# Two reordered attention blocks with half of their zero products, and a third whose exponentials read PSUM

## The reference, cut to what matters

```
# layers 0 and 2: 16 heads of 8 dimensions, keys and values from the 77 context tokens
Q = (x @ Wq.T).reshape(B, xN, 16, 8)
attn = softmax(einsum('bqhd,bkhd->bhqk', Q, K) * SCALE)
O = einsum('bhqk,bkhd->bqhd', attn, V).reshape(B, xN, 128)
return O @ Wo.T

# layer 3, first attention: 16 heads of 32 dimensions, keys and values from x itself (128 tokens)
a = softmax(einsum('bhsd,bhtd->bhst', q, k) * D ** (-0.5))
a = a * mask          # after the softmax: later keys only
o = einsum('bhst,bhtd->bhsd', a, v)
x_out = x + o @ li1_w + li1_b
```

## Time and profile before

| what | value |
|---|---|
| median of 3 runs | 5575.47 us (5569.66 to 5575.83) |
| the profiled execution's own time | 5589.97 us |
| its span, first to last instruction | 5588.1 us |
| busy, share of the span: PE, PEld | 87%, 64% |
| busy: DVE, ACT, POOL | 71%, 48%, 39% |
| mean granted TensorE clock | 0.936 of full speed |

### The profile page before, as it was taken

The page is one execution under the profiler, slowest core; times in us unless marked ns, Lnnn a source line. Parts: engine busy times, 40 slices in busy tenths (PEclk is TensorE's granted clock), DMA queues, the critical chain, the costliest instruction groups (busy, mean ns, idle before and its releaser), DMA issues. The chain is left out here.

```text
span 5588.1 us, 132733 instructions
## 1 busy us (share of the span) xinstructions
PE 4842.0 (87%) x41659; PEld 3572.6 (64%) x41659; DVE 3953.4 (71%) x9897; ACT 2700.3 (48%) x5454; POOL 2176.0 (39%) x3095
## 2 busy tenths in 40 slices
PE   7888998999952799688889989889898899998898
PEld 4555667888852466455566667767776677776554
DVE  5666876777766333677767768989886789897544
ACT  4545774555530233454555545555553455554344
POOL 5443001100027100776533357777776433333200
PEclk9989999999975899899999999999998999999878
DMA  1002400000011333100100000000000000000000
GB/s 40 8 7 66 209 0 6 5 5 5 5 56 44 114 135 133 35 23 22 30 2 0 0 6 0 0 0 0 0 0 7 3 2 2 2 2 7 0 14 17
DMA packets 109012, 141.38 MB, mean 25 GB/s; under 512 B 35832, under 2 KB 83256, under 8 KB 103996
## 3 DMA queue, kind: packets, MB, share of 16 engines
q1 hardware_dynamic: 100544, 120.88, 6.3%
q0 software_dynamic: 8192, 16.79, 1.0%
HBM read 47.44 MB, written 58.72 MB: 19 GB/s over the span
## 5 line engine op out<-in xcount | busy, mean ns | idle before, releaser
L2213 POOL TENSOR_TENSOR l3a_probs<-l3a_probs,l3a_later 128x512 f32<-128x512 f32 x256 | 320.6, 1280 | 4.9 <-DVE l3a_total L2401 4.9
L2199 POOL TENSOR_TENSOR l3a_keys<-l3a_kT,head 128x2048 f32<-128x2048 f32 x64 | 230.4, 3600 | 232.2 <-ACT l3a_kT L2326 232.2
L181 POOL TENSOR_TENSOR l1x_ve<-l1x_mv,eps 128x1 f32<-128x1 f32 x64 | 12.2, 190 | 646.7 <-DVE l1x_mv L173 646.7
L2261 PE MATMUL l3a_scores<-l3a_keys,l3a_qT 128*128 128x512 f32 x512 | 255.5, 601 | 4.2 <-POOL l3a_keys L2199 4.2
L1696 POOL TENSOR_TENSOR l2f_hid<-l2f_prod,l2f_route 128x512 f32<-128x512 f32 x128 | 152.1, 1193 | 254.7 <-DVE l2f_prod L1843 251.3
L309 PE MATMUL l3a_po<-l3a_vals,l3a_probsT 128*128 128x32 f32 x2048 | 251.0, 271 | 0.1
L309 PEld LDWEIGHTS l3a_po<-l3a_vals,l3a_probsT 128*128 128x128 f32 x2048 | 250.2, 194 | 0.4 <-ACT l3a_probsT L290 0.4
L265 ACT ACTIVATE l3a_probs<-l3a_probs 128x512 f32<-128x512 f32 x256 | 161.7, 632 | 180.7 <-DVE l3a_probs L256 175.7
L1582 PE MATMUL l1e_h<-l1e_xhi,l1f_parts 128*128 128x512 f16 x640 | 205.1, 382 | 9.7 <-DVE l1e_gated L1640 8.2
L2199 POOL TENSOR_TENSOR l3c_keys<-l3c_kT,head 128x1232 f32<-128x1232 f32 x64 | 144.0, 2250 | 156.7 <-ACT l3c_kT L2326 156.7
L295 DVE SCALAR_TENSOR_TENSOR l1x_loT<-l1x_turned,l1x_hiT 77x512 f16<-77x512 f32 x256 | 168.9, 679 | 48.9 <-ACT l1x_hiT L288 48.9
(11 more groups left out here) (581 smaller groups left out, 17155.9 us busy)
## 6 DMA issues: line engine op xcount, KB each, us to landing
l_rows<-l0f_zeros SPq DMA_DIRECT2D x34, 1024.0 KB, 27.1
l1f_parts<-l1f_split SPq DMA_DIRECT2D x40, 512.0 KB, 3.6
l1e_x_in<-l_rows SPq DMA_DIRECT2D x40, 256.0 KB, 2.8
l1f_down<-l1f_w SPq DMA_DIRECT2D x40, 256.0 KB, 2.4
l_rows<-l1e_y_out SPq DMA_DIRECT2D x40, 256.0 KB, 2.7
l1f_w<-in_L_W SPq DMA_DIRECT2D x16, 256.0 KB, 3.6
out_x<-x_res SPq DMA_DIRECT2D x16, 256.0 KB, 2.0
x_res<-in_x SPq DMA_DIRECT2D x1, 3840.0 KB, 12.3
```

The lines of the kernel that those rows point to most:

```text
L2199: pool.tensor_tensor(keys[it.par][:, :, :, :], kT[it.par][:, :, :].unsqueeze(2).to_broadcast([P, J, G4, T]), g.head32[:, :].unsqueeze(1).u ...
L2213: pool.tensor_tensor(v, v, later[:, :].unsqueeze(1).to_broadcast([P, 4, T]), ALU.mult).then_inc(s_masked, 1)
L2261: pe.matmul(scores[c][:, 0:G4 * T], qT[it.par][:, c, :], keys[it.par][:, c, :, :].rearrange("p h t -> p (h t)"), start=True, stop=True).th ...
```

## The change

It has two parts.

1. In both 8-dimension attentions the lists of GpSimd, TensorE, ScalarE and VectorE are written in another order, with other lags, and a product with zeros follows only pieces 0, 2, 4 and 6 of a batch: four a batch, where there were eight.
2. In the first attention of layer 3 the shift is left out. ScalarE makes the exponentials from the scores in PSUM, one instruction for each head (128 columns) with that head's maximum as its bias column; the scores come out of TensorE with the scale and a minus sign in them, so VectorE takes minima. The scores' bank is free after the exponentials. VectorE's list loses its four shifts and has `sum0` and `sum1` earlier.

```diff
+    def exponential_of_bank(self, act, it, c):
+        a, b = self.first[c], self.first[c + 1]
+        act.wait_ge(self.s_max, nth(it, self.nb, c))
+        if (due := nth(it, self.nc_, ago=2)) is not None:
+            act.wait_ge(self.s_turn, due)
+        for h in range(a, b):
+            last = act.activation(self.probs[it.par][:, h, :], self.view(c)[:, h - a, :], ACT.Exp,
+                                  bias=self.mx[it.par][:, h:h + 1], scale=-1.0)
+        last.then_inc(self.s_exp, 1)
...
-                        if u < 2:
+                        if c < 8 and c % 2 == 0:
 
                             pe.matmul(po[:, HEADS * E1:BANK], blank[:, 0:P], blank[:, HEADS * E1:BANK], start=False, stop=False,
...
-                order = ["weigh2-2 scoreA shiftB-1 turn0-1 turn_o-2 v1 output-2 scoreB turn1-1 turn2-1 mtA weigh0-1 shiftA mtB weigh1-1",
+                order = ["shiftB-1 turn0-1 scoreA turn_o-2 v1 output-2 scoreB mtA turn1-1 turn2-1 shiftA weigh0-1 mtB x weigh1-1 weigh2-1",
...
-                order = ["mB-1 expB-1 o-2 high0-1 v0 high1-1 high2-1 mA expA",
+                order = ["expB-1 high0-1 o-2 c mA high1-1 high2-1 expA mB x",
...
-                order = ["rest2-2 v0 row0-2 divide-2 maxA row1-2 add-2 rest0-1 maxB rest1-1",
+                order = ["divide-2 maxA rest0-1 add-2 row0-1 maxB v1 rest1-1 rest2-1 row1-1 stats",
...
-        sm = Softmax(st, g, scores, [4] * 4, T, scale, turned, split=not first)
+        sm = Softmax(st, g, scores, [4] * 4, T, scale, turned, split=not first, direct=first)
...
-                        pe.wait_ge(sm.s_shift, due)
+                        pe.wait_ge(sm.s_exp if first else sm.s_shift, due)
...
+                    if first:
+                        act.activation(dst, pa[:, :], ACT.Copy, scale=-scale).then_inc(s_qT, 1)
...
-                    names = ("hat stats3 maximum0 stats2 shift0 maximum1 add shift1 maximum2 maximum3 shift2 shift3 sum0 "
-                             "sum1 stats1 sum2 sum3 divide")
+                    names = "hat stats3 maximum0 stats2 maximum1 add sum0 maximum2 sum1 maximum3 stats1 sum2 sum3 divide"
```

More of the change, by code:

```diff
@@ L213, with __init__ @@
 class Softmax:
-    def __init__(self, st, g, banks, heads_of_bank, keys, scale, ps_turn, split=False):
+    def __init__(self, st, g, banks, heads_of_bank, keys, scale, ps_turn, split=False, direct=False):
+        self.direct = direct
         self.g, self.banks, self.keys, self.scale = g, banks, keys, scale
@@ L745, in _ @@
                     steps["rows"] = gather
-                lags = {"s1": 2, "value0": 2, "s2": 2, "bias": 2, "value1": 2, "s3": 2, "deviation": 0, "rest": 1, "next": 1, "rows": -1}
-                order = ["maxA s1 value0 maxB s2 rows",
-                         "bias maxA maxB value1 rows s3",
+                lags = {"deviation": 0, "rest": 1, "next": 1, "value0": 1, "rows": -1}
+                order = ["maxA maxB s1 rows",
+                         "bias maxA s2 maxB value1 s3 rows",
                          "maxA deviation maxB rest rows",
-                         "maxA maxB next rows"]
+                         "next maxA maxB value0 rows"]
                 skewed(pool, n, slots(steps, lags, order), n if routed else 6)
@@ L2319, in fetch_q @@
                         act.wait_ge(sm.s_scores, due)
[L2320 removed]
+                    dst = qT[it.par][:, :, :].rearrange("p j t -> p (j t)")
+                    if first:
+                        act.activation(dst, pa[:, :], ACT.Copy, scale=-scale).then_inc(s_qT, 1)
+                    else:
+                        act.copy(dst, pa[:, :]).then_inc(s_qT, 1)
                 def fetch_k(it):
@@ L2345, in _ @@
                 steps = {**numbered("fetch_p", lambda it, c: sm.fetch(act, it, c), 4, 5),
-                         **numbered("exp", lambda it, c: sm.exponential(act, it, c), 4, 4), "fetch_x": (fetch_x, 3),
+                         **numbered("exp", lambda it, c: (sm.exponential_of_bank if first else sm.exponential)(act, it, c), 4, 4), "fetch_x": (fetch_x, 3),
                          "fetch_q": (fetch_q, 3), "fetch_k": (fetch_k, 3), "fetch_v": (fetch_v, 3), "fetch_o": (fetch_o, 6)}
@@ L2425, in _ @@
                 steps = {**numbered("maximum", lambda it, c: sm.maximum(dve, it, c), 4, 4),
-                         **numbered("shift", lambda it, c: sm.shift(dve, it, c), 4, 4), **numbered("sum", row_sum, 4, 4),
+                         **numbered("sum", row_sum, 4, 4),
                          "hat": (hat, 3 if first else 2), "divide": (divide, 5 if first else 6), "add": (add, 6)}
```

12 lines of the change are left out of this document (6 added, 6 removed), and 18 rows, old and new, of the table order.

## The result

The changed kernel takes 5589.2 us (median of 11 runs, 5582.6 to 5605.3), the kernel before in the same session 5577.3 us (11 runs). The ratio is 1.0025, with a 95% interval of 1.0014 to 1.0036. The forecast was 5495 us, the range 5420 to 5600, "slower" had 0.16.

The account below looks back on a forecast made before the run. It took TensorE to bound `l0x`, TensorE and VectorE both near the limit in `l2x`, and VectorE to bound `l3a`. Part 1 (-22 us) and part 2 (-60) took the 5575.47 median to 5493, stated as 5495 us, range 5420 to 5600.

Parts of the forecast that it names:

- Three terms: Forecast stage changes, clock falls included: `l0x` -18 us, `l2x` -4 us, `l3a` -60 us.
- the prediction's own signs: Clock under 0.8 in `l0x` or `l2x` would show the clock rival; `l3a` over 14.3 us a batch, a wrong forecast.
- the clock rival: `l0x` and `l2x`: fewer zeros make the clock fall more; 5735 us, or 5650 if half as bad; chance 0.15.
- The zeros' price: `l0x` and `l2x`: each product with zeros costs 0.16 us on TensorE; four fewer a batch gain at most 40 us a stage.
- The new waiting in `l0x`: The new order adds 0.1 to 0.4 us of waiting a batch, taken as 0.2; `l0x` gains 27 us before clock falls.
- The two idle stretches at the loop's boundary stay: `l0x`: TensorE's idle 3.63 and 2.48 us at each loop turn were assumed to remain, so no gain there.
- The clock in `l2x`: Four more falls to half clock in `l2x`, 4.5 us each, giving back 18 us.
- the clock takes it back: Full name of the clock rival: half clock at 60% of `l0x` and `l2x` gives 5735 us; chance 0.15.
- The order in `l2x`: New waiting in `l2x` taken as 0.35 us a batch, leaving a 22 us gain; waits expected at VectorE's rest (`s_lo`).
- Part 2's prices: `l3a`: 0.36 us per 128-column exponential, about 1.2 a bank; wait before keys goes, 0.5 us new; 60 us gained.
- GpSimd's order and passes are unchanged: `l3a`: GpSimd was taken as unaffected by part 2, busy 10.6 us a batch, with no cost added.
- ScalarE bounds `l3a`: Slower exponentials, or VectorE's SBUF passes meeting GpSimd, cut part 2 to 0 to -20 us; 5540 us; chance 0.15.

Follow-up runs that it names:

- e5: Kernel before plus 80 already fulfilled waits (40 instructions) at the start of TensorE's list of `l0x`; ratio 0.9923, 5557.3 us.
- e1: Kernel before with four instead of eight products with zeros a batch in both 8-dimension attentions, old lists kept; ratio 0.9835, 5485.9 us.
- e2: Kernel before with the new lists in both 8-dimension attentions, all eight zeros kept, `l3a` as before; ratio 1.0003.
- e10: The changed kernel, unchanged, measured and profiled again beside the kernel before; ratio 1.0022.
- e9: The kernel before, unchanged, measured and profiled again; ratio 0.9999.
- e11: The changed kernel with VectorE adding the experts' rows one slot later in `l2x`, in one session with the changed kernel; ratio 1.0088.
- e13: Kernel before with six zeros in `l0x`; new lists, later rows, eight zeros, moved loop in `l2x`; part 2, mask on one head of four; ratio 0.9858.
- e12: Kernel before with four zeros in `l0x`, eight in `l2x` behind 80 fulfilled waits, old lists, and part 2; ratio 0.9813, 5470.9 us.
- e3: Kernel before with only part 2, `l3a`'s exponentials from PSUM; ratio 0.9988.
- e15: e12 with VectorE's affine passes and statistics in `l3a` moved behind the maxima of banks 0 and 1, whole mask kept; ratio 0.9801, 5460.0 us.
- e17: e15 with ScalarE's exponentials of bank 3 behind its copy of the last probabilities in `l3a`; ratio 0.9771.
- e16: e15 with two zeros a batch in `l0x` instead of four; ratio 0.9817.
- e7: The changed kernel with VectorE adding the experts' rows one slot later in `l2x`, in an earlier session; ratio 1.0044.
- e6: e1 plus part 2, `l3a`'s exponentials from PSUM; ratio 0.9896.
- e8: Kernel before with no zeros in `l0x`, eight in `l2x` with its loop moved by 40 instructions, old lists; ratio 0.9971.

## Why the prediction was wrong, point by point

The forecast was a gain, and the kernel lost 0.25%. Three terms were off by about as much each: `l0x` came out 43 us better than forecast, `l2x` 54 and `l3a` 51 us worse. That 5589 lies inside the stated range is luck, since one miss hid half of the two others. Two of the prediction's own signs say the same: it named 0.8 as the clock in `l2x` under which the clock rival holds (it was 0.76), and 14.3 us a batch in `l3a` as the mark of being wrong (the mean was 14.4).

**The zeros' price: right, a little high.** I had 0.16 us each, at most 40 us for four fewer a batch. With nothing loaded and no fall, `l0x` went from 464 to 432 us (e5, e1), 32 us or 0.125 each.

**The new waiting in `l0x`: right in size, in part by luck.** I took 0.2 us a batch. Old and new lists at four zeros differ by 445 - 432 = 13 us, 0.20 a batch, but 10 of the 445 us ran at half clock, which is some 5 of the 13. At eight zeros, with no time at half clock in either, they differ by 467.4 - 463.8 = 3.6 us (e2, e5), 0.06 a batch.

**"The two idle stretches at the loop's boundary stay": the step that failed in `l0x`.** I had read the earlier trace rows as a property of the loop. They came with loads of instructions, and they went: 41 us by e5. With them went the stays at half clock behind them. Forecast -18, measured -61 and -47 (e10 against e9; in e10 the first three batches took 10 us each).

**The clock in `l2x`: the step that failed there.** I took four more falls at 4.5 us, 18 us. The clock fell 14 times where it had fallen 6 times, and behind the first fall of the stage each stay lasted 14 to 24 us where it had been 7 to 17. Time at half clock went from 92 to 314 us; at half of the work lost in it, an estimate, that is 111 us instead of 18. By the same estimate the rest of the stage got some 60 us shorter, by the fewer zeros and by the loads, which ended in this loop as in that of `l0x`. So without the clock the stage would have been a gain. The rival *the clock takes it back* had assumed 60% of the stage at half clock; it was 53% (after) and 59% (e10), in this stage alone. So that rival came true in one of its two stages. I gave it 0.15 because I joined the two stages: in `l0x`, where TensorE bounds, four zeros are enough, and in `l2x`, where VectorE was close behind, they are not. The earlier trace rows had that difference. The earlier trace rows had the sign, a fall at 81% busy.

The rule of the Trainium skill that I weighed (TensorE: Matmul & The Clock Gate, "HAM oscillation": idle gaps throttle) could not be applied as a sum of gaps here: with later rows (e11) TensorE's waits in the window fell from 21.4 to 17.4 us, and it ran at half clock for longer. Read for single gaps the traces agree with it in the new lists: e11's window has nine waits for the division of 1.8 us each where e10's has mostly waits of 0.6, and in e13 14 of 15 waits of over 0.85 us had a fall. With the old lists (e12) ten such waits had none.

**The order in `l2x`: the mechanism was right in kind, not in place.** This is the second part of what failed there. I looked for the wait at VectorE's rest (`s_lo`), and it is 0.2 us at most. New were the waits for the gathered rows and for GpSimd's maxima, since `row0-2` had become `row0-1`. That was in the diff and I costed it at nothing. But removing them (e11) brought no time; what was left was the wait for the division. At eight zeros the new lists, with the later rows, cost 52 us (e13 against e12), at four, as they stand in the change, 66 (e10 against e1, two sessions). Four fewer zeros cost 20 us with the old lists (e1 against e12) where I had counted a gain. The two together take the stage from 507 to 593 us.

**Part 2's prices: right.** I had 0.36 us an exponential and 1.2 a bank; the lines by form of after give

```profile
L275 ACT ACTIVATE l3a_probs<-l3a_scores,l3a_mx 128x128 f32<-128x128 f32 x1024 | 299.6, 399 | 43.8 <-DVE l3a_mx L249 43.0
```

and TensorE's waits in the stage

```profile
PE l3a_po L321 <- ACT l3a_probsT L302: 26.2, 63, 0.4
PE l3a_pa L2261 <- ACT l3a_qT L2334: 14.8, 30, 1.8
```

0.40 by itself, and a bank's four took 1.15 from the first start to the last end (3605.85 to 3607.00 in e3). The new wait ahead of the last sum is 0.4 us (I had 0.5), the old one before the keys fell from 1.49 in the earlier trace rows (87.1 us in all) to 14.8 / 64 = 0.23 a batch.

**"GpSimd's order and passes are unchanged": the step that failed in `l3a`.** They are, but VectorE's passes moved under them. One more affine pass met the mask, 308 to 772 ns in the mean, in every other batch 1.35 us. In those batches the first minima end late, the queries' copy behind them, and the batch takes 14.5 us; in the others 13.5 (13.6 was forecast). The clock fell 16 times in the stage instead of twice, mostly for 3.4 us, 74 us at half instead of 38. This is the second half of the rival *ScalarE bounds `l3a`*, with its 0 to -20 us and its 0.15. With three quarters of the mask pass left out (e13) the stage is 55 us shorter than before, against 60 forecast, and the new bound is TensorE. e13 does not price the new collision by itself: it shortens GpSimd's own work, and it also frees the passes that had been long before the change (840 and 1324 ns there); e15 did not remove it, and no run did that with the whole mask in place. That ScalarE's order counts as well is shown by e17: 28 us less than e16 in this stage, with the passes as slow as ever. My sum had the wait that went there at 0.5 us (0.4 measured) and took it as given.

**`l3f`** moved by +13 in the profiled pair without an edit. It took from 299 to 329 us over the kernels here, with 98 to 172 at half clock; the kernel before itself took 315.8 and 305.2 us (e9). It was 322 to 329 in all four profiles with the new lists and four zeros in `l2x` (after, e7, e10, e11), and 299 to 316 in all others. So part of the change's loss, 13 to 17 us, arises there, and the cause stays open.

## What to carry to other kernels

Before costing any edit of TensorE's list, compare the rows of the loading queue over a loop's stretch: a loop that loads its instructions again at each turn pays for it (41 us in one stage here), and any edit ahead of it, even one that does nothing, can start or stop that. Judge filler products stage by stage, by the time at half clock and not by the busy share: in these two stages two to four were enough where TensorE bounds, eight were better than four where VectorE is close, and with four taking away one wait made the stage longer. Look at the length of single waits, and not only at their sum. When an engine is relieved, ask which of its remaining SBUF passes slide under another engine's long one, and when one pass is moved out, add up all of them: others may have slid in.

## What the runs showed of the hardware that I had not expected

- Instructions are loaded by a queue that the page counts: 177 packets before, 112 to 114 where both loops stay. While it ran in the loop (9 packets a turn), TensorE stood with "issue" as its releaser, 3.63 and 2.48 us a turn, and a stay at half clock followed; e5 took all three away together.
- VectorE passes of 128x128 over SBUF took 0.29 us when they started ahead of GpSimd's mask pass, and up to 1.35 (e12) when they started inside it; the minima, which read PSUM, kept theirs (0.682 in the mean before, 0.686 after).
- In two of the sessions (before: medians of 5598.8 and 5605.3 instead of 5574 to 5577) `l2x` was longer with the same instructions: 557 us in e17, 509 in e15. The other stages agreed but for `l3a` in e6. In e17, 38 of the 128 exponentials of `l2x` started over 0.6 us after the product that they needed had ended, and 33 to 42 in e5, e6, e8 and e16 of these two sessions; in e12 and e15 one did. One chip had sessions of both kinds. The traces name no cause.
